# Cross-attention in a three-stage decoder block: scores issued in one stretch, maxima subtracted inside the second by-key block, projection behind the shift, gelus first

## The chip, the cores and the metric

One core of one Trainium2 chip. The metric is the device time of the whole program in microseconds (us); for the kernel before it is the median of three runs.

## The reference, cut to what matters

A decoder layer on `x` [64, 128, 128] with the context `ctx` [64, 77, 128], all in float32: self-attention, cross-attention, and an expert feed-forward network, each behind a layernorm and added to `x`. The change is in the cross-attention alone:

```python
def xattn(query, key, value, ...):            # query: layernorm(x), key = value: ctx
    Q, K, V = linear(query, Wq, bq), linear(key, Wk, bk), linear(value, Wv, bv)   # 16 heads of 8
    qk = einsum('bhqd,bhkd->bhqk', Q, K)
    scores = qk / sqrt(dk)
    mean_sim = scores.mean(axis=(-2, -1))
    max_sim = scores.max(axis=-1).mean(axis=-1)
    probs = softmax(scores, axis=-1)
    entropy_proxy = var(probs, axis=-1, ddof=1).mean(axis=-1)
    feats = stack([mean_sim, max_sim, entropy_proxy], axis=-1)
    hidden = gelu(linear(feats, w1, b1)); hidden = gelu(linear(hidden, w2, b2))
    t = exp(clip(linear(hidden, w3, b3), LOG_T_MIN, LOG_T_MAX))[..., None]
    attn = softmax(qk / (2.0 * t), axis=-1)
    return linear(einsum('bhqk,bhkd->bhqd', attn, V), Wo, bo)
```

So every head of every batch needs its scores twice: once for three features, from which a small MLP makes a temperature, and once with that temperature for the attention proper.

## The kernel before, in words

The three stages run one after the other. In the cross-attention one batch (128 queries by 77 keys, 16 heads) is a work item, and a software pipeline runs over the steps `n` of `STEPS`. In step `n` the engines work on these batches, with `LAG` = 7:

- batch `n + 2`: transposes of the normalised `x` and of the context (`xc_transpose`), the products Q, K and V (`qkv`), and their copies on ACT (`qkv_copy`) and casts on DVE (`cast`) and POOL (`low`, `key_masks`);
- batch `n`: first scores, queries on partitions, in the PSUM tile `SQ` of three banks (`scores_outer`, `scores_inner`), row maxima on DVE (`row_max`), their transpose (`max_transpose`), negated on ACT (`mT_copy`), subtracted in PSUM by three matmuls (`subtract_max`), exponentials on ACT (`exp_e`), sums on DVE;
- batch `n - 7`: second scores, keys on partitions, in `SK` of two banks, eight heads at a time (`by_key(b, 0)` and `by_key(b, 1)`): two matmuls put in the shift (`pick`, `shift`), six add the products; then the exponential on ACT (`exps(b, h)`, into `P`) and the product with V (`pv(b, h)`);
- batch `n - 8`: `o_copy`, `o_transpose`, `norm`, `on_transpose`, `onT_copy`;
- batch `n - 9`: `project` (bias matmul and output matrix) and `residual`.

`SK` exists once. So `by_key(b, 1)` waits for `exps(b, 0)`, and `by_key(b + 1, 0)` for `exps(b, 1)`: `need(pe, p_ready, 2 * b + h)`, L1273. `SQ` exists once as well; `scores_outer` waits for the exponentials of the batch before (`e1_ready`).

Once in four steps (`mlp_round(n)`, n = 5, 9, ..., 65) the MLP of four batches runs: `mlp1`, `gelu1`, `mlp2`, `gelu2`, `mlp3`, `bound`, `inverse_t`, `factors`. Exponential and gelu need different tables in ACT, so that such a step has two table loads.

Every product in float32 is made of three parts (high by high, high by low, low by high). The scores' matmuls use 32 of the 128 rows: group `g` of four heads lies on rows `32g` to `32g + 31` of the keys and queries (masked per head). The 16 heads stand in `SQ` six, six and four to a bank, so that heads 4 to 7 are cut into two pieces, and the outer groups write heads 0 to 3, 8 to 11 and 12 to 15. The inner ones may start only behind them (`outer_ps`), since the first matmul into a bank clears its flags.

The order of the work on each engine is written out by hand in the loop over `STEPS` at the end of each engine's block; PE takes its instructions from one queue, and each function's waits stand at its head. While the pipeline fills (n from 2 to 6) and at its end (n from 64), `filler` puts matmuls without a use on PE.

## Time and profile before

| | us |
|---|---|
| median of three runs | 1720.15 (1714.52 to 1722.27) |
| the profiled execution | 1719.28 |
| its span | 1717.5 |
| cross-attention, by the first transposes on PE and the last projection | from 484.5 to 1159.9 |

| engine | busy us | share of the span |
|---|---|---|
| PE (matmul) | 1642.8 | 96% |
| DVE | 1235.7 | 72% |
| ACT | 926.2 | 54% |
| POOL | 880.2 | 51% |

A share is an average over three stages. To read the change, one looks at the cross-attention alone, at one step and at one round of four steps, and at which wait ends last there. PE's ends are modelled, so a busy PE may still hold gaps; the starts of its rows tell more than its busy time. The granted clock of TensorE is 1.0 at full speed (2.4 GHz) and 0.5 at half (1.2 GHz).

### The profile page before, as it was taken

The page shows a single profiled execution, that of the slowest core. Times are in us where ns is not written, and L with a number is a line of the kernel's source. Part 1 is how long each engine was busy: PE and PEld are TensorE (multiplying, and loading weights), DVE is VectorE, ACT ScalarE, POOL GpSimd, SP SyncE. Part 2 cuts the span into 40 slices and gives each one's busy share as a digit, 9 for nine tenths or more (in the row PEclk, how much of TensorE's full clock was granted, in tenths as well). Part 3 has the DMA queues.
Part 4 walks back from the last instruction along what each step waited for, and adds up shares of the span by engine and source line. Part 5 has one row for each costly group of instructions (what it writes and reads, how often), then busy time and mean ns, then how long its engine had stood idle before and what let it go on. Part 6 is the DMA issues. An engine that isn't in the chain of part 4 may idle for free. (4 is left out here: it accounts for less than half of the span.)

```text
span 1717.5 us, 42620 instructions
## 1 busy us (share of the span) xinstructions
PE 1642.8 (96%) x14336; PEld 1223.2 (71%) x14336; DVE 1235.7 (72%) x2888; ACT 926.2 (54%) x2189; POOL 880.2 (51%) x1006
## 2 busy tenths in 40 slices
PE   6999999999978999999999999897999999999998
PEld 2555555555546666666666666557999999999998
DVE  5887777777646767766677776436878878787886
ACT  3555545555433666666566666545454545545452
POOL 3444455544446767776677777412433434343342
PEclk9999999999958999998999999788999999999999
DMA  4000000000000000000000000100000000000000
GB/s 123 13 3 2 1 1 1 1 1 1 6 5 4 7 7 7 6 7 6 6 7 7 7 7 5 43 2 1 11 6 9 6 9 6 9 9 6 9 6 13
DMA packets 27869, 16.62 MB, mean 10 GB/s; under 512 B 6193, under 2 KB 25586, under 8 KB 27762
## 3 DMA queue, kind: packets, MB, share of 16 engines
q1 hardware_dynamic: 27762, 15.23, 3.2%
q8 instruction: 63, 1.03, 0.3%
q14 instruction: 44, 0.36, 0.1%
HBM read 9.97 MB, written 4.19 MB: 8 GB/s over the span
## 5 line engine op out<-in xcount | busy, mean ns | idle before, releaser
L1555 POOL TENSOR_TENSOR ff_zz<-ff_zt 128x256 f32<-128x256 f32 x32 | 37.5, 1173 | 318.2 <-DVE ff_zt L1759 318.2
L278 POOL TENSOR_TENSOR sa_KM<-sa_HQK,sc_headmask 128x512 fp32r<-128x512 f32 x64 | 66.7, 1042 | 235.6 <-ACT sa_HQK L318 235.6
L964 ACT ACTIVATE xa_P<-xa_SK 77x1024 f32<-77x1024 f32 x128 | 130.2, 1017 | 98.1 <-PE xa_SK L1287 97.9
L1623 ACT ACTIVATE ff_SG<-bank 128x512 f32<-128x512 f32 x128 | 76.6, 599 | 189.3 <-PE bank L1836 189.3
L1749 DVE TENSOR_TENSOR ff_GL<-ff_GU,ff_GH 128x512 fp32r<-128x512 f32 x128 | 148.6, 1180 | 27.2 <-ACT ff_GH L1628 27.2
L323 ACT ACTIVATE sa_P<-sa_SK 128x1024 f32<-128x1024 f32 x128 | 131.5, 1028 | 59.1 <-PE sa_SK L515 59.1
L409 DVE TENSOR_REDUCE sa_mx<-sa_SQ 128x8 f32<-128x1024 f32 x128 | 156.7, 1224 | 7.6 <-PE sa_SQ L515 5.3
L890 POOL TENSOR_TENSOR xa_QMH<-xa_QBH,xc_headmask 128x512 fp32r<-128x512 f32 x64 | 72.6, 1135 | 151.2 <-ACT xa_QBH L954 151.2
L1901 PE MATMUL bank<-fh_r,ff_GH 128*128 128x256 f32 x512 | 149.2, 292 | 0.0
L1834 PE MATMUL bank<-ff_ZH,fh_b 128*128 128x256 f32 x512 | 146.2, 286 | 0.0
L1903 PE MATMUL bank<-fh_r,ff_GL 128*128 128x256 f32 x512 | 144.5, 282 | 0.0
L1902 PE MATMUL bank<-fl_r,ff_GH 128*128 128x256 f32 x512 | 144.4, 282 | 0.0
L1836 PE MATMUL bank<-ff_ZH,fl_b 128*128 128x256 f32 x512 | 143.8, 281 | 0.0
L1835 PE MATMUL bank<-ff_ZL,fh_b 128*128 128x256 f32 x512 | 143.2, 280 | 0.0
L849 POOL TENSOR_TENSOR xa_E<-xa_E 128x1232 f32<-128x1232 f32 x64 | 143.2, 2238 | 0.0
L1744 DVE TENSOR_TENSOR ff_GU<-ff_SG,bank 128x512 f32<-128x512 f32 x128 | 88.1, 688 | 64.4 <-ACT ff_SG L1623 58.7
L1628 ACT CAST ff_GH<-ff_GU 128x512 fp32r<-128x512 f32 x128 | 79.0, 623 | 56.3 <-DVE ff_GU L1744 33.1
L1080 DVE TENSOR_REDUCE xa_FEAT<-xa_SQ 128x12 f32<-128x924 f32 x64 | 71.7, 1120 | 42.0 <-PE xa_SQ L1236 41.7
L1563 POOL TENSOR_TENSOR ff_ZH<-ff_AH,ff_M 128x512 fp32r<-128x512 f32 x64 | 83.4, 1303 | 34.3 <-ACT ff_M L1601 34.3
L534 PE MATMUL sa_SK<-sa_shift,sa_pick_row 128*128 128x512 f32 x256 | 99.9, 471 | 0.7 <-ACT sa_P L323 0.6
L1902 PEld LDWEIGHTS bank<-fl_r,ff_GH 128*128 128x128 f32 x512 | 97.4, 190 | 0.0
L1901 PEld LDWEIGHTS bank<-fh_r,ff_GH 128*128 128x128 f32 x512 | 97.2, 190 | 0.0
(259 smaller groups left out, 5398.3 us busy)
## 6 DMA issues: line engine op xcount, KB each, us to landing
xa_shift<-xa_row SPq DMA_DIRECT2D x256, 2.0 KB
out<-X SPq DMA_DIRECT2D x64, 64.0 KB, 1.5
cx<-ctx SPq DMA_DIRECT2D x64, 38.5 KB
sa_shift<-sa_mT SPq DMA_DIRECT2D x64, 8.0 KB, 1.8
X<-x SPq DMA_DIRECT2D x1, 768.0 KB, 6.7
xa_E<-L_ffn_B SPq DMA_DIRECT2D x2, 256.0 KB, 3.7
xa_E<-down_a SPq DMA_DIRECT2D x1, 512.0 KB, 4.4
X<-x SPq DMA_DIRECT2D x1, 256.0 KB, 2.9
```

What stands on the lines that cost most here:

```text
L323: nc.scalar.activation(P[:, 2 * (k % 2) + h, :], SK[:], ACT.Exp).then_inc(p_ready, 1)
L409: nc.vector.tensor_reduce(mx[:, p, 2 * JH * h:2 * JH * h + 2 * JH], SQ[:].rearrange("q (j k) -> q j k", k=T), AX.X, ALU.max).then_inc(max_ ...
L534: mm(bank(SK, a), pick_row[:], shift[:, k % 2, JH * g:JH * g + JH, :].rearrange("c j t -> c (j t)"), start=True, stop=False)
L849: nc.gpsimd.tensor_tensor(E2[:], E1[:, b % 2], E1[:, b % 2], ALU.mult).then_inc(e2_ready, 1)
L964: nc.scalar.activation(P[0:TC, (2 * b + h) % 4, :], SK[0:TC, :], ACT.Exp).then_inc(p_ready, 1)
L1749: nc.vector.tensor_tensor(GG[1][:, k % 4, :], GU[:, k % 2, :], GG[0][:, k % 4, :].bitcast(F32), ALU.subtract).then_inc(gl_done, 1)
L1834: mm(out, w[0], x[0], start=start, stop=False, **kw)
L1835: mm(out, w[0], x[1], start=False, stop=False, **kw)
L1836: return mm(out, w[1], x[0], start=False, stop=stop, **kw)
L1901: mm(out, h, RD[0][:, f, :], start=(s == 0 and f == 0), stop=False, skip_group_check=True)
L1902: mm(out, h, RD[1][:, f, :], start=False, stop=False, skip_group_check=True)
L1903: last = mm(out, l, RD[0][:, f, :], start=False, stop=(s == 1 and f == 3), skip_group_check=True)
```

## The change

- The constant `CROSS_ORDER` = (2, 1, 3, 0) gives the group of heads that stands at each place of `SQ`. Groups 2 and 3 are now the first and third place, group 1 is the one cut in two, and group 0 has the last bank. `headsel` and the four rows of the shift that SP copies are put in the same order; the number of DMAs stays at four.
- PE: the first scores are one stretch. `scores_outer` holds places 0 and 2 (six matmuls), `scores_inner` begins with the first matmul of place 3, waits for `outer_ps`, and holds the other eight. It moves ahead of the transposes of batch `n + 2`.
- PE: `pv(n - 8, 1)` moves from behind the outer scores to behind those transposes; `project` from the head of the step into `by_key(n - 7, 0)`, behind its shift matmuls; `max_transpose` out of `by_key(n - 7, 1)` to ahead of it; `subtract_max` into it, behind its shift matmuls.
- PE: `mlp1`, `mlp2` and `mlp3` stand behind the scores, behind the transposes and behind `pv(n - 8, 1)`.
- ACT: in a step with MLP both gelus stand ahead of `exps(n - 7, 0)`; in every step `scaled` is first, and `exp_e` and `onT_copy` stand ahead of `exps(n - 7, 1)`.
- DVE: `residual` behind `sum_e`, `bound` ahead of `stats`, `layernorm` ahead of `cast`, `factors` ahead of `sum_e2`, `norm` at one place in all steps.
- The fillers of a step while the pipeline fills: four, three and two where it had four and six.

```diff
+CROSS_ORDER = (2, 1, 3, 0)
...
-                for g in range(QUADS):
+                for place, g in enumerate(ORDER):
                     sp.dma_start(shift[32 * g:32 * g + 1, b % 2].bitcast(F32),
-                                 row[JH * g:JH * g + JH].bitcast(F32)).then_inc(m_row[b % 2], 16)
+                                 row[JH * place:JH * place + JH].bitcast(F32)).then_inc(m_row[b % 2], 16)
...
                 r = mlp_round(n)
-                if real(n - LAG):
-                    exps(n - LAG, 0)
                 if real(n - LAG + 1):
                     scaled(n - LAG + 1)
+                if r is not None:
+                    gelu1(r)
+                if real(n - LAG) and r is None:
+                    exps(n - LAG, 0)
                 if real(n + 2):
                     xcT_copy(n + 2)
                 if r is not None:
-                    gelu1(r)
+                    gelu2(r)
                 if real(n - LAG - 1):
                     o_copy(n - LAG - 1)
-                if r is not None:
-                    gelu2(r)
+                if real(n - LAG) and r is not None:
+                    exps(n - LAG, 0)
                 if real(n):
                     mT_copy(n)
                 if real(n + 2):
                     qkv_copy(n + 2)
+                if r is not None:
+                    inverse_t(r)
+                if real(n):
+                    exp_e(n)
+                if real(n - LAG - 1):
+                    onT_copy(n - LAG - 1)
                 if real(n - LAG):
                     exps(n - LAG, 1)
-                if r is not None:
-                    inverse_t(r)
-                if real(n - LAG - 1):
-                    onT_copy(n - LAG - 1)
-                if real(n):
-                    exp_e(n)
...
                 for part in range(3):
-                    scores(b, 0, 4, part, part == 0, part == 2)
-                    scores(b, 8, 12, part, part == 0, part == 2)
-                    last = scores(b, 12, 16, part, part == 0, part == 2)
+                    scores(b, 0, 4, part)
+                    last = scores(b, 8, 12, part)
                 last.then_inc(outer_ps, 1)
 
             def scores_inner(b):
+                scores(b, 12, 16, 0)
                 pe.wait_ge(outer_ps, b + 1)
                 for part in range(3):
-                    scores(b, 4, 6, part, False, part == 2)
-                    last = scores(b, 6, 8, part, False, part == 2)
+                    if part > 0:
+                        scores(b, 12, 16, part)
+                    scores(b, 4, 6, part)
+                    last = scores(b, 6, 8, part)
                 last.then_inc(sq_ps, 1)
...
                 for a, _, r in quads:
                     mm(bank(SK, a), pick[:, r // 32], shift[:, b % 2].rearrange("c j t -> c (j t)"),
                        start=True, stop=False)
+                between()
                 for part, (keys, queries) in enumerate(((HK, QMH), (HK, QML), (LK, QMH))):
...
-                if real(n - LAG - 2):
-                    project(n - LAG - 2)
...
                 if real(n - LAG):
-                    by_key(n - LAG, 0)
+                    by_key(n - LAG, 0, project_last)
+                else:
+                    project_last()
                 if real(n):
                     scores_outer(n)
-                if real(n - LAG - 1):
-                    pv(n - LAG - 1, 1)
+                    scores_inner(n)
                 if r is not None:
                     mlp1(r, n)
                 if real(n + 2):
                     xc_transpose(n + 2)
-                if real(n):
-                    scores_inner(n)
+                if r is not None:
+                    mlp2(r)
+                if real(n - LAG - 1):
+                    pv(n - LAG - 1, 1)
+                elif 2 <= n < LAG:
+                    filler(SK[:, 512:1024], 3)
+                if r is not None:
+                    mlp3(r)
                 if real(n + 2):
                     qkv(n + 2)
...
+                if real(n):
+                    max_transpose(n)
                 if real(n - LAG):
-                    by_key(n - LAG, 1, maxima)
+                    by_key(n - LAG, 1, subtract)
```

Where the instructions stand now, first on PE, in a step without MLP of the steady part: around the second by-key block (into `xa_SK`). Before, from the transposes of o (`o_transpose`, into `xa_R`) to the projection:

```order
L1321 MATMUL xa_R<-fc_ident,xa_o 128x128 x2
L1283 MATMUL xa_SK<-xa_shift,xa_pick 128x512 x2
L1287 MATMUL xa_SK<-xa_QMH,xa_HK 128x512 x2
L1261 MATMUL xa_O<-fc_ident,xa_FEAT 16x128
L1287 MATMUL xa_SK<-xa_QML,xa_HK 128x512 x2
L1287 MATMUL xa_SK<-xa_QMH,xa_LK 128x512 x2
L1268 MATMUL xa_SQ<-xa_heads,xa_mT 128x462 x2
L1268 MATMUL xa_SQ<-xa_heads,xa_mT 128x308
L1326 MATMUL xa_R<-fc_ident,xa_on 128x128
L1305 MATMUL xa_O<-xa_P,xa_VA 32x128 x8
L1333 MATMUL xa_M<-xa_bias,xa_minus_ones 128x128
L1334 MATMUL xa_M<-xc_wo,xa_onT 128x128
```

With the change, from behind those transposes to the projection inside the next step's block:

```order
L1267 MATMUL xa_O<-fc_ident,xa_FEAT 16x128
L1289 MATMUL xa_SK<-xa_shift,xa_pick 128x512 x2
L1274 MATMUL xa_SQ<-xa_heads,xa_mT 128x462 x2
L1274 MATMUL xa_SQ<-xa_heads,xa_mT 128x308
L1294 MATMUL xa_SK<-xa_QMH,xa_HK 128x512 x2
L1294 MATMUL xa_SK<-xa_QML,xa_HK 128x512 x2
L1294 MATMUL xa_SK<-xa_QMH,xa_LK 128x512 x2
L1331 MATMUL xa_R<-fc_ident,xa_on 128x128
L1310 MATMUL xa_O<-xa_P,xa_VA 32x128 x8
L1289 MATMUL xa_SK<-xa_shift,xa_pick 128x512 x2
L1338 MATMUL xa_M<-xa_bias,xa_minus_ones 128x128
L1339 MATMUL xa_M<-xc_wo,xa_onT 128x128
```

The transpose of the maxima (into `xa_O`) left the block and stands ahead of it, the three subtracting matmuls (into `xa_SQ`) moved in behind the shift, and the projection (into `xa_M`) moved from between `pv` and the next block to behind that block's shift.

Then the first scores (into `xa_SQ`) of the same kind of step on PE, from the last row of `by_key(n - 7, 0)`. Before:

```order
L1287 MATMUL xa_SK<-xa_QMH,xa_LK 128x512 x2
L1236 MATMUL xa_SQ<-xa_KMH,xa_HQ 128x308 x3
L1236 MATMUL xa_SQ<-xa_KML,xa_HQ 128x308 x3
L1236 MATMUL xa_SQ<-xa_KMH,xa_LQ 128x308 x3
L1305 MATMUL xa_O<-xa_P,xa_VA 32x128 x8
L1217 MATMUL xa_M<-fc_ident,xa_xn 128x128
L1218 MATMUL xa_M<-fc_ident,cx 128x77
L1236 MATMUL xa_SQ<-xa_KMH,xa_HQ 128x154 x2
L1236 MATMUL xa_SQ<-xa_KML,xa_HQ 128x154 x2
L1236 MATMUL xa_SQ<-xa_KMH,xa_LQ 128x154 x2
```

With the change:

```order
L1294 MATMUL xa_SK<-xa_QMH,xa_LK 128x512 x2
L1240 MATMUL xa_SQ<-xa_KMH,xa_HQ 128x308 x2
L1240 MATMUL xa_SQ<-xa_KML,xa_HQ 128x308 x2
L1240 MATMUL xa_SQ<-xa_KMH,xa_LQ 128x308 x2
L1240 MATMUL xa_SQ<-xa_KMH,xa_HQ 128x308
L1240 MATMUL xa_SQ<-xa_KMH,xa_HQ 128x154 x2
L1240 MATMUL xa_SQ<-xa_KML,xa_HQ 128x308
L1240 MATMUL xa_SQ<-xa_KML,xa_HQ 128x154 x2
L1240 MATMUL xa_SQ<-xa_KMH,xa_LQ 128x308
L1240 MATMUL xa_SQ<-xa_KMH,xa_LQ 128x154 x2
L1221 MATMUL xa_M<-fc_ident,xa_xn 128x128
L1222 MATMUL xa_M<-fc_ident,cx 128x77
```

The 15 matmuls stand together, with those of group 0 (the last place, 308 columns) between those of group 1 (154 columns each); `pv` and the transposes follow them.

And ACT in a step with MLP, from its first instruction on. Before:

```order
L964 ACTIVATE xa_P<-xa_SK 77x1024
L954 ACTIVATE xa_QBH<-xa_QK,xa_cfc 128x128
L957 ACTIVATE xa_row<-xa_mT,xa_cfh 16x128
L915 COPY xa_xcT<-xa_M 128x205
L978 ACT_TABLE_LOAD
L978 ACTIVATE xa_h<-xa_R,xa_b1s 64x64
L969 COPY xa_o<-xa_O 128x256
L982 ACTIVATE xa_h<-xa_R,xc_b 64x64
L937 ACTIVATE xa_mT<-xa_O 16x128
L922 ACTIVATE xa_QK,xa_qsum<-xa_M,xc_bq 128x128
L924 ACTIVATE xa_QK,xa_ksum<-xa_M,xc_bk 128x77
L931 COPY xa_VA<-xa_M 77x2x8x8
```

With the change:

```order
L958 ACTIVATE xa_QBH<-xa_QK,xa_cfc 128x128
L961 ACTIVATE xa_row<-xa_mT,xa_cfh 16x128
L982 ACT_TABLE_LOAD
L982 ACTIVATE xa_h<-xa_R,xa_b1s 64x64
L919 COPY xa_xcT<-xa_M 128x205
L986 ACTIVATE xa_h<-xa_R,xc_b 64x64
L973 COPY xa_o<-xa_O 128x256
L968 ACT_TABLE_LOAD
L968 ACTIVATE xa_P<-xa_SK 77x1024
L941 ACTIVATE xa_mT<-xa_O 16x128
L926 ACTIVATE xa_QK,xa_qsum<-xa_M,xc_bq 128x128
L928 ACTIVATE xa_QK,xa_ksum<-xa_M,xc_bk 128x77
```

Both gelus (`xa_h`) stand ahead of the first exponential of `SK` (`xa_P`), and the second one is behind the exponentials of `SQ` (`xa_E`) and the copy `xa_onT`, of which the rows above show all but the end.

## Rows read from the trace of the kernel before

**Rows 1.** One round: length, busy us of PE, PEld, DVE, ACT, POOL; granted clock.

```profile
852.29:889.53 37.24, 35.61 (x335) 23.91 (x335) 26.85 (x57) 24.91 (x66) 27.09 (x34) 1.00 0.03 7
```

**Rows 2.** PE in order of time, three places: start us, us, engine, line, operation.

```profile
584.15 0.32 PE L1333 MATMUL xa_M<-xa_bias,xa_minus_ones 2*128 2x128 f32 x1 [0.77 <-ACT xa_onT L974]
...
695.18 1.38 PE L1268 MATMUL xa_SQ<-xa_heads,xa_mT 128*128 128x462 f32 x3
...
1076.58 0.47 PE L1333 MATMUL xa_M<-xa_bias,xa_minus_ones 2*128 2x128 f32 x1
```

**Rows 3.** PE in order of time, one step without MLP (899.24 to 906.69).

```profile
899.24 0.50 PE L1287 MATMUL xa_SK<-xa_QMH,xa_HK 32*128 32x512 f32 x2
899.35 0.41 PE L1236 MATMUL xa_SQ<-xa_KMH,xa_HQ 32*128 32x308 f32 x2
899.58 0.40 PE L1287 MATMUL xa_SK<-xa_QML,xa_HK 32*128 32x512 f32 x2
...
899.83 0.39 PE L1236 MATMUL xa_SQ<-xa_KMH,xa_LQ 32*128 32x308 f32 x2
...
900.55 0.64 PE L1305 MATMUL xa_O<-xa_P,xa_VA 128*32 128x128 f32 x16
...
901.45 0.45 PE L1236 MATMUL xa_SQ<-xa_KMH,xa_HQ 32*128 32x154 f32 x2
...
902.27 0.49 PE L1222 MATMUL xa_M<-xa_xcT,xc_wq 128*128 128x128 f32 x2
...
903.14 0.70 PE L1283 MATMUL xa_SK<-xa_shift,xa_pick 128*128 128x512 f32 x2
...
904.20 0.28 PE L1261 MATMUL xa_O<-fc_ident,xa_FEAT 128*16 128x128 f32 x1
904.41 0.50 PE L1287 MATMUL xa_SK<-xa_QML,xa_HK 32*128 32x512 f32 x2
...
905.07 0.83 PE L1268 MATMUL xa_SQ<-xa_heads,xa_mT 128*128 128x462 f32 x3
905.74 0.27 PE L1326 MATMUL xa_R<-fc_ident,xa_on 128*128 128x128 f32 x1
...
906.69 0.32 PE L1333 MATMUL xa_M<-xa_bias,xa_minus_ones 2*128 2x128 f32 x1
```

**Rows 4.** ACT in order of time, the end of the same step.

```profile
906.40 0.24 ACT L974 COPY xa_onT<-xa_R 128x128 f32<-128x128 f32 x1
...
907.38 0.40 ACT L946 ACTIVATE xa_E<-xa_SQ 128x308 f32<-128x308 f32 x1
```

**Rows 5.** PE in order of time, a by-key block alone, behind the last scores.

```profile
1138.31 0.70 PE L1283 MATMUL xa_SK<-xa_shift,xa_pick 128*128 128x512 f32 x2
...
1139.83 0.33 PE L1326 MATMUL xa_R<-fc_ident,xa_on 128*128 128x128 f32 x1
```

**Rows 6.** PE and ACT in order of time, the step with MLP at 881.

```profile
881.08 0.56 PE L1344 MATMUL xa_R<-xa_FEAT,xa_w1s 128*64 128x64 f32 x6
...
882.36 1.28 ACT L978 ACT_TABLE_LOAD   x1
...
883.65 0.31 ACT L978 ACTIVATE xa_h<-xa_R,xa_b1s 64x64 f32<-64x64 f32 x1
...
883.86 0.35 ACT L969 COPY xa_o<-xa_O 128x256 f32<-128x256 f32 x1
...
884.01 0.43 PE L1349 MATMUL xa_R<-xa_h,xa_w2p 64*128 64x64 f32 x2 [0.40 <-ACT xa_h L978]
...
889.53 0.32 PE L1333 MATMUL xa_M<-xa_bias,xa_minus_ones 2*128 2x128 f32 x1 [0.81 <-ACT xa_onT L974]
```

**Rows 7.** ACT in order of time, the last step with MLP, where ACT waits.

```profile
1110.61 1.28 ACT L964 ACT_TABLE_LOAD   x1
1113.05 1.02 ACT L964 ACTIVATE xa_P<-xa_SK 77x1024 f32<-77x1024 f32 x1 [1.16 <-PE xa_SK L1287]
```

**Rows 8.** PE in order of time, the first step with MLP, while the pipeline fills.

```profile
539.31 0.90 PE L1344 MATMUL xa_R<-xa_FEAT,xa_w1s 128*64 128x64 f32 x6 [2.51 <-POOL xa_FEAT L869]
```

65 lines of the change are left out of this document (29 added, 36 removed).

## The prediction

> **What bounds the kernel now.** The page of the profile says PE 96% busy over the span. The stretches by stage are read next. In one undisturbed round of four steps PE is busy 35.61 of 37.24 us, the next engine, POOL, 27.09 [rows 1]; DVE and ACT lie near it. So PE's one queue sets the pace, and the others count only where PE waits for them. Then PE in order of time: a step without MLP takes 8.58 (889.53 to 906.69 are two) [rows 3, 6], and it has almost no gap. The round leaves 37.24 - 3 x 8.58 = 11.50 for the step with MLP, whose gaps the list of waits names: 0.40 for the first gelu and 0.81 for the copy `onT` [rows 6]. So the change is read on PE's queue: which instructions get closer together, and which of PE's new places is reached before the result it needs.
>
> The sum is made against the profiled execution, 1719.28 (span 1717.5), 0.9 under the median 1720.15. I reckon one step, from the end of one by-key block to the end of the next, and multiply: steps 7 to 63 are full, 14 of them with MLP and 43 without.
>
> **a. Scores in one stretch.** Before, from the first product of `by_key(b, 0)` to `pv` 1.31 (899.24 to 900.55), and the inner scores 0.82 (901.45 to 902.27): 2.13 [rows 3]. The first is that long because group 0 of the scores shares its rows with the by-key block and comes last. Now groups 2 and 3 run beside the block: such a pair starts at 899.35, 0.11 behind the block's first, the last pair at 899.83 with 0.39 to its end, 900.22 [rows 3]. The inner scores must wait for that end; before, `pv` and the transposes covered it. With 0.05 for the semaphore (a gelu ends at 883.96, its matmul starts at 884.01 [rows 6]) they start at 900.27 and take 0.82; group 0's matmuls run on other rows beside group 1's. So 899.24 to 901.09, 1.85: **-0.28**. Bounds: nothing gained, 2.13 (0); or no wait and a tighter pace, 1.65 (-0.48: start at 900.05, half the gaps of group 1 filled, 0.84). I take 1.85, since its two parts are rows.
>
> The trace shows scores starting (899.35) ahead of the second by-key product (899.58), which stands before them in the program [rows 3]. The Trainium skill, TensorE: Matmul & The Clock Gate, section "Part 3: Packing small matmuls", says that matmuls start and end strictly in program order, whatever their row groups. By that the pairs would queue up behind the block and the stretch would give nothing; the trace disagrees, and the measurement decides.
>
> **b. Maxima out of the second block.** Before, from its shift to the subtraction 1.93 (903.14 to 905.07), with the transpose of the maxima inside, which waits for both row groups to run empty [rows 3]. A block alone takes 1.52 (1138.31 to 1139.83) [rows 5]. The transpose itself still costs 0.21 (904.20 to 904.41) [rows 3]. 1.52 + 0.21 - 1.93 = **-0.20**. The subtraction only changes its place. Is the transpose reached too early? From the inner scores to it were 2.75 us (901.45 to 904.20) [rows 3]; now transposes 0.33, `pv` 0.57, `qkv` with `o_transpose` 0.87 and the 0.82 themselves give 2.59. A wait of up to 0.16 is possible; the 2.75 were partly the drain, so I book none.
>
> **c. Projection behind the shift.** The same instructions in another order, one change to 32 rows either way: 0. Its wait for `onT` goes.
>
> **d. What is late next.** The shift of `by_key(b + 1, 0)` overwrites `SK` and needs `exps(b, 1)`. Before, ACT did that exponential at once behind the block, and subtraction, `on_transpose`, `pv` and projection covered it. Now ACT has `exp_e` and `onT_copy` ahead of it, and PE has only `on_transpose` and one `pv` to do. The chain from the start of `on_transpose`: 0.27 [rows 3], 0.05, the copy 0.24 [rows 4], the exponential 1.02 [rows 7] less 0.10 of overlap (a copy starts at 883.86, 0.10 ahead of the end of the gelu [rows 6]), 0.05: 1.53. Before, from `on_transpose` to the next instruction 0.95 (905.74 to 906.69) [rows 3]. **+0.58** a step; PE stands still for some 0.75 of it. `exp_e` itself fits between: copy and both its parts take 1.38 (906.40 to 907.78) [rows 4], so 1.24 from the end of the subtraction, while the products of the block take 0.89 and `on_transpose` 0.3. ACT's order here undoes what a and b save.
>
> Step without MLP: -0.28 - 0.20 + 0.58 = +0.10, so 8.68; 43 x 0.10 = **+4.3**.
>
> **e. Step with MLP.** Add to 8.68: `mlp1` 0.56; the first gelu, 0.05 + 0.31 + 0.05 behind it, of which the transposes cover 0.33: 0.08; `mlp2` 0.43 [rows 6], `mlp3` as much. The gelu's table load of 1.28 [rows 6] is now hidden: a load does not wait for its instruction's semaphore (at 1110.61 it ran at once, its exponential waited for PE until 1113.05 [rows 7]), and ACT is idle there until the MLP starts. The other load moves ahead of `exps(b, 0)`, and the second block's shift waits for that: from the end of `pv`, ACT needs 0.05 + 0.35 (copy of o) + 1.28 + 1.02 + 0.05 = 2.75, PE has `mlp3` 0.43, 0.87 and 0.21 to do; a stall of 1.24. Together 8.68 + 1.50 + 1.24 = 11.42 against 11.50; 14 x -0.08 = **-1.1**. One stall has taken the place of the two.
>
> **f. Filling and emptying.** Seven steps without by-key: the scores' saving holds, 7 x -0.28 = -2. In step 5 PE stood 2.51 before `mlp1` [rows 8], and the inner scores behind it; now they are ahead: -2.5. The ten steps behind the last scores hold the same chain d: +1. The fillers are 5 instead of 6 in the middle of a step and cost nothing, since PE waits there. DVE's new order: it has 26.85 of 37.24 us to do [rows 1]; SP's DMAs keep number and place: 0. **-3.5**.
>
> **g. Clock.** The 13 rounds from 584.15 to 1076.58 take 492.4 [rows 2], 13 x 37.24 are 484.1: 8.3 more than the undisturbed round gives. In such rounds rows stand at half speed at the end of the step with MLP: the subtraction at 695.18 shows 1.38 where 905.07 has 0.83 [rows 2, 3]. PE had waited before it, and matmuls of 64 columns ran. With the MLP in one run and its weak stretch broken up by `pv`, I estimate that half of it goes: **-4**, with -8 and the rival below as its bounds.
>
> The Trainium skill, same page, section "Part 1: The HAM clock gate", puts the half rate down to a stretch in which the engine was idle. By that the kernel before would lose nothing, for no gap in a round exceeds 0.81 [rows 6], and g would be 0. The rows disagree.
>
> Sum: 4.3 - 1.1 - 3.5 - 4 = -4.3, so 1719.3 - 4.3 = **1715**.
>
> **The rivals.**
> - **The scores pack tighter (faster).** If the stretch takes 1.65 instead of 1.85, 57 x -0.20 = -11.4: **1704**. For it: pairs of different groups start 0.11 apart, and group 1 alone leaves gaps. Against it: the wait for `outer_ps` is now in the open.
> - **Half clock on the path (slower).** PE's standstill of 1.24 is followed by subtraction, block and `on_transpose`, which all lie on chain d. At half speed the subtraction takes 0.55 more [rows 2, 3] and the rest about as much again by its 0.89: 1.2 a round, where before the wait for `onT` hid most of it. 15 rounds give 18, and the 4 of g are lost as well: **1737**. It decides where most rounds have it. For it: the step holds one gap longer than any before, and each step a second one of 0.75. Against it: `pv`, with full rows, stands right before the gap.
> - **No overlap in the stretch (slower).** Groups 0 and 1 take turns or the wait is long: 2.13, so +0.28 x 57 = 16: **1731**. By the page's rule of program order it would be this one; the pairs at 899.35 speak against it.
>
> **How the numbers follow.** Forecast 0.46, first rival 0.29, second 0.17, third 0.08. A measurement tells about 0.5% from no change, 8.6 us: faster is under 1711.5, slower over 1728.7. The forecast's own spread (0.16 of a wait in b, 0.05 here or there in d, a few us of clock) is 1709 to 1723; a little of it is faster, and the first rival nearly all: 0.32. The second and third give slower, less some that stop short: 0.22. Same: 0.46. The range reaches from below the first rival, with the clock's gain on top, to just short of the second: 1700 to 1735; some 2 in 10, mostly half clock, lie outside.
>
> **What the profile after would show.** Steps without MLP of 8.68; PE's shift at the head of a step waiting some 0.75 for `xa_P` (`exps(b, 1)`); in the step with MLP one wait of 1.2 for `xa_P` at the second block, and no wait above 0.2 for a gelu; from the first by-key product to the transposes of `x` 1.85. A step of 8.5 or less with 1.65 there is the first rival, 8.9 with 2.1 the third; subtractions of 1.38 in most rounds the second. If PE shows no wait for `xa_P` at the head of a step, d is wrong, and with it the forecast: it would then be some 30 us too high.

## The result and the profile after

| | before | after |
|---|---|---|
| median | 1720.15 (beside the changed kernel 1720.8) | 1777.01 |
| runs | 1714.52 to 1722.27 | 1776.23, 1755.99, 1802.93, 1777.79 |
| profiled execution | 1719.28, span 1717.5 | 1776.23, span 1774.4 |

The ratio of after to before is 1.0293, with a 95% interval of 1.02 to 1.0387: slower, by something between 2 and 4%. The forecast was 1715, its range 1700 to 1735; the time lies 42 above the range. A run over 1.5% above the fastest of its kernel, like that of 1802.93, is not part of a ratio, here and below.

The page of the profile of the changed kernel: span, busy times, and the granted clock in 40 slices of the span (tenths).

```profile
span 1774.4 us, 42623 instructions
...
PE 1664.5 (94%) x14337; PEld 1239.6 (70%) x14337; DVE 1231.9 (69%) x2888; ACT 941.9 (53%) x2189; POOL 872.8 (49%) x1006
...
PEclk9999999999968799999798888897999999999999
```

PE has 94% instead of 96%, and the clock row holds 6, 7 and 8 in ten slices between the 12th and the 28th, where the cross-attention runs. Two causes are possible, then: the order and the clock. The stretches tell them apart. First one undisturbed round of the changed kernel (the answer to [rows 1]), then a stretch of 560 us in the middle of the cross-attention, then a piece of it; the columns are those of [rows 1], with the granted clock after the engines:

```profile
896.75:935.47 38.72, 34.54 (x335) 23.19 (x335) 26.19 (x56) 25.98 (x65) 26.58 (x35) 1.00 0.03 7
...
560.00:1120.00 560.00, 514.02 (x4432) 346.65 (x4432) 349.29 (x743) 346.66 (x867) 355.25 (x455) 0.88 0.02 6
...
994.00:1011.10 17.10, 16.39 (x91) 11.35 (x91) 7.75 (x20) 8.04 (x18) 6.29 (x7) 0.50 0.01 3
```

The same 560 us of the kernel before:

```profile
560.00:1120.00 560.00, 542.69 (x4843) 362.40 (x4842) 383.08 (x803) 360.41 (x925) 388.16 (x484) 0.94 0.03 9
```

The round takes 38.72 instead of 37.24 us at full clock, with 34.54 instead of 35.61 of PE busy. And the mean clock is 0.88 against 0.94: half-speed time is twice the missing part, (1 - 0.88) x 2 x 560 = 134 us against 67. The trace's own record of the clock gives 133 and 70 for the same 560 us, and where half-speed time is given from here on, it is from that record and for these 560 us of the profiled execution. It comes in whole spells, as from 994.0 to 1011.1, where the clock is 0.50 throughout.

PE in order of time at either end of 13 rounds, as in [rows 2]:

```profile
587.32 0.47 PE L1338 MATMUL xa_M<-xa_bias,xa_minus_ones 2*128 2x128 f32 x1
...
1136.19 0.47 PE L1338 MATMUL xa_M<-xa_bias,xa_minus_ones 2*128 2x128 f32 x1
```

That is 548.9 us; before it was 492.4. An undisturbed round, one at full clock throughout, is 11.76 + 3 x 8.99 = 38.73 (the one above has 38.72). Of the +56.5, 13 x (38.73 - 37.24) = **+19.4 is the order**, and what is left, **+37.1, the clock**: 548.9 stands 45.4 above 13 undisturbed rounds, before it was 8.3. The spans differ by 56.9, so all that lies outside these 13 rounds changed by 0.4.

The size of the clock's part holds for the profiled execution alone. Its mean clock is 0.936 over the whole span; the run of 1755.99 had 0.955, close to the 0.957 of the profiled execution before, and still took 37 us longer than that one. Half-speed time is also dearer in this kernel: within the 13 rounds 132 us of it cost 45.4, before 51 us cost 8.3.

**Where the spells begin.** `mlp1` starts at 991.49 in the round of the spell above, and the clock falls 2.4 us later. PE behind the fall, at the second by-key block:

```profile
996.27 1.22 PE L1289 MATMUL xa_SK<-xa_shift,xa_pick 128*128 128x512 f32 x2 [0.46 <-ACT xa_P L968]
```

So in this round the wait for `exps(b, 0)` comes 2 us behind the fall and can't have brought it. Six of the eleven spells that begin in the 560 us (92 of the 133 us) start in this way, 1.4 to 2.5 us behind the start of `mlp1`; the other five start at other places.

**A step without MLP**, PE in order of time (it answers to [rows 3]):

```profile
926.49 0.32 PE L1338 MATMUL xa_M<-xa_bias,xa_minus_ones 2*128 2x128 f32 x1
...
927.16 0.50 PE L1294 MATMUL xa_SK<-xa_QMH,xa_HK 32*128 32x512 f32 x2
927.18 0.41 PE L1240 MATMUL xa_SQ<-xa_KMH,xa_HQ 32*128 32x308 f32 x2
...
927.50 0.39 PE L1294 MATMUL xa_SK<-xa_QML,xa_HK 32*128 32x512 f32 x2
927.57 0.30 PE L1240 MATMUL xa_SQ<-xa_KMH,xa_LQ 32*128 32x308 f32 x2
...
928.27 0.40 PE L1240 MATMUL xa_SQ<-xa_KML,xa_HQ 32*128 32x308 f32 x1
...
929.09 0.33 PE L1221 MATMUL xa_M<-fc_ident,xa_xn 128*128 128x128 f32 x1
...
930.71 0.38 PE L1326 MATMUL xa_R<-fc_ident,xa_o 128*128 128x128 f32 x2
...
930.96 0.71 PE L1289 MATMUL xa_SK<-xa_shift,xa_pick 128*128 128x512 f32 x2
931.56 0.82 PE L1274 MATMUL xa_SQ<-xa_heads,xa_mT 128*128 128x462 f32 x3
...
933.20 0.33 PE L1331 MATMUL xa_R<-fc_ident,xa_on 128*128 128x128 f32 x1
...
934.80 0.74 PE L1289 MATMUL xa_SK<-xa_shift,xa_pick 128*128 128x512 f32 x2 [0.70 <-ACT xa_P L968]
935.47 0.32 PE L1338 MATMUL xa_M<-xa_bias,xa_minus_ones 2*128 2x128 f32 x1
```

935.47 - 926.49 = 8.98 (8.97 to 9.00 in the undisturbed steps without MLP) where the forecast was 8.68 and before 8.58. In pieces, before against after:

| piece | before | after | change | forecast |
|---|---|---|---|---|
| by-key and all scores | 1.31 + 0.82 | 1.93 (927.16 to 929.09) | -0.20 | -0.28 |
| `o_transpose` to `on_transpose`: maxima, second block, subtraction | 2.74 | 2.49 (930.71 to 933.20) | -0.25 | -0.20 |
| `project` and the first shift | 1.12 | 0.66 + 0.67 | +0.21 | 0 |
| `on_transpose` to the next head | 0.95 | 1.60 (933.20 to 934.80) | +0.65 | +0.58 |

The row of the third piece in the kernel before, the shift and the first product behind `project` (906.69, [rows 3]):

```profile
907.18 0.70 PE L1283 MATMUL xa_SK<-xa_shift,xa_pick 128*128 128x512 f32 x2
907.81 0.50 PE L1287 MATMUL xa_SK<-xa_QMH,xa_HK 32*128 32x512 f32 x2
```

The wait at the head is in the list of waits (total us, times, longest; 700 to 1150 us), with the MLP steps' larger one in the same row:

```profile
PE xa_SK L1289 <- ACT xa_P L968: 34.7, 52, 1.3
```

Of the 52, 37 are of 0.70 and 4 of 1.31; the other 11, of 0.3 to 0.5, stand where PE runs at half speed and so comes later.

ACT in order of time at the end of that step shows the chain behind it: the two parts of `exp_e` (the first is shown), the copy `onT`, `exps(b, 1)`.

```profile
932.42 0.94 ACT L949 ACTIVATE xa_E<-xa_SQ 128x924 f32<-128x924 f32 x1
...
933.57 0.27 ACT L978 COPY xa_onT<-xa_R 128x128 f32<-128x128 f32 x1
933.73 1.02 ACT L968 ACTIVATE xa_P<-xa_SK 77x1024 f32<-77x1024 f32 x1
```

**The step with MLP** at 905.74 takes 11.76 (before 11.50). ACT, in order of time (it answers to [rows 6]); then PE at the second by-key block:

```profile
905.61 1.28 ACT L982 ACT_TABLE_LOAD   x1
908.93 0.31 ACT L982 ACTIVATE xa_h<-xa_R,xa_b1s 64x64 f32<-64x64 f32 x1 [2.03 <-PE xa_R L1349]
...
910.75 1.28 ACT L968 ACT_TABLE_LOAD   x1
912.04 1.02 ACT L968 ACTIVATE xa_P<-xa_SK 77x1024 f32<-77x1024 f32 x1
```

```profile
911.53 0.27 PE L1267 MATMUL xa_O<-fc_ident,xa_FEAT 128*16 128x128 f32 x1
913.12 0.73 PE L1289 MATMUL xa_SK<-xa_shift,xa_pick 128*128 128x512 f32 x2 [1.31 <-ACT xa_P L968]
```

The gelu's table load runs at 905.61, while ACT waits for `mlp1` anyway, and the list of PE's waits has none for a gelu any more. The second load stands ahead of `exps(b, 0)`, and PE waits 1.31 for that exponential.

### The profile page after: what moved, and what is told of

The parts are those of the page before. It is cut to its first block and busy times, and to the rows that moved or that the text cites. A ratio compares the mean times of both kernels' runs of the same rounds, so it can differ in the third digit from the quotient of the medians.

```text
span 1774.4 us, 42623 instructions
## 1 busy us (share of the span) xinstructions
PE 1664.5 (94%) x14337; PEld 1239.6 (70%) x14337; DVE 1231.9 (69%) x2888; ACT 941.9 (53%) x2189; POOL 872.8 (49%) x1006
## 5 line engine op out<-in xcount | busy, mean ns | idle before, releaser
L1289 PE MATMUL xa_SK<-xa_shift,xa_pick 128*128 128x512 f32 x256 | 103.1, 487 | 52.4 <-ACT xa_P L968 51.4
L878 POOL TENSOR_TENSOR xa_LK<-xa_QK,xa_HK 128x77 fp32r<-128x77 f32 x64 | 21.7, 340 | 164.3 <-DVE xa_HQ L1079 164.3
L1289 PEld LDWEIGHTS xa_SK<-xa_shift,xa_pick 128*128 128x128 f32 x256 | 43.3, 212 | 77.8 <-ACT xa_P L968 75.4
```

Source lines behind the costliest of these rows:

```text
L1289: mm(bank(SK, a), pick[:, r // 32], shift[:, b % 2].rearrange("c j t -> c (j t)"), start=True, stop=False)
```

## The experiments

Fifteen kernels ran, in four lots, each beside the kernel before (whose medians in these were 1716.8, 1714.6, 1721.6 and 1720.0). Times are medians, with the ratio to before. First those that undo one part, on the changed kernel.

**e1: projection back at the head of its step.**

```diff
+                project_last()
...
                 if real(n - LAG):
-                    by_key(n - LAG, 0, project_last)
-                else:
-                    project_last()
+                    by_key(n - LAG, 0, lambda: None)
```

> The changed kernel with one thing undone: the projection stands again at the head of the step, ahead of the first by-key block, not behind its shift. Theory A (the order costs 0.4 a step because the exponential exps(b, 1) comes late, PE has nothing to do meanwhile, and the projection inside the block costs 0.49 plus a drain of 0.18 on the path): the projection moves into the wait of 0.70, steps without MLP go from 8.98 to 8.31, a round from 38.7 to 36.1, so some 13 x 2.6 = 34 us less than the changed kernel, and 1705 to 1740 by what the clock does. Theory B (the clock alone is the loss): the steps at full clock matter little, the spells at half speed stay, about 1770. Rival C (the scores in one stretch are the loss): steps stay near 8.9.

Measured 1703.8, 0.995 (0.9896 to 1.0003). The step is 8.31 or 8.32, as worked out, the MLP step 11.10. PE in order of time, from `on_transpose` over `project` and the shift to the first product:

```profile
932.15 0.33 PE L1331 MATMUL xa_R<-fc_ident,xa_on 128*128 128x128 f32 x1
...
932.99 0.32 PE L1338 MATMUL xa_M<-xa_bias,xa_minus_ones 2*128 2x128 f32 x1
...
933.76 0.74 PE L1289 MATMUL xa_SK<-xa_shift,xa_pick 128*128 128x512 f32 x2
934.42 0.49 PE L1294 MATMUL xa_SK<-xa_QMH,xa_HK 32*128 32x512 f32 x2
```

That is 2.27, against 2.93 in the changed kernel (933.20 to 936.14) and 2.07 before: the matmuls of `project` now stand where PE waited for `exps(b, 1)`, and nothing stands between shift and products. So `project` in this place costs 0.66 a step. Part c, booked at nothing, is 0.21 of it; the other 0.45 is wait that `project` no longer covers, and that was in the price of d. Half-speed time is 58 us. The list of waits:

```profile
PE xa_SK L1289 <- ACT xa_P L968: 15.1, 12, 1.3
```

Eleven of the twelve waits left are the MLP steps' stall (1.31). It is as long as in the changed kernel, and yet the record of the clock has five spells instead of eleven. Against the kernel before, e1 is not clear of noise: its interval reaches 1.

**e2: ACT does `exps(b, 1)` first, then `onT`, then `exp_e`** (the order before). **e3: both edits.**

```diff
+                if real(n - LAG):
+                    exps(n - LAG, 1)
+                if real(n - LAG - 1):
+                    onT_copy(n - LAG - 1)
                 if real(n):
                     exp_e(n)
-                if real(n - LAG - 1):
-                    onT_copy(n - LAG - 1)
-                if real(n - LAG):
-                    exps(n - LAG, 1)
```

> The changed kernel with another thing undone: on ACT exps(n - 7, 1), onT_copy, exp_e in the order of the kernel before. Theory A: from the start of on_transpose to the next shift 1.19 (0.12 + 1.02 + 0.05) where it is 1.60, so 0.41 less a step, 8.57, and 20 to 25 us less than the changed kernel at equal clock. Theory B: no change beyond the clock's scatter, about 1770. If exp_e comes too late for the next scores, part of the 0.41 comes back as a wait of the scores.

> Both undone at once: projection at the head of the step and ACT's old order. Theory A: the projection now waits for onT_copy, which stands behind the exponential, from the start of on_transpose 1.04 + 0.24 + 0.05 = 1.33, then 0.66 of projection: 1.99 to the shift, where the first of the two alone has 1.60; steps of 8.7, so slower than the projection alone by 0.4 a step, near the kernel before, 1720 to 1730. If two parts of a loss simply added, it would be the fastest of the three.

e2: 1736.8, 1.0139 (1.0077 to 1.02), step 8.57, half-speed time 81 us. The head's wait falls from 0.70 to 0.28. e3: 1718.6, 1.0003 (0.9985 to 1.002), step 8.52. There PE waits for the other copy, at `project`:

```profile
933.65 0.32 PE L1338 MATMUL xa_M<-xa_bias,xa_minus_ones 2*128 2x128 f32 x1 [0.43 <-ACT xa_onT L978]
```

So d is real, but ACT's old order helps only where the projection stands inside the block. With the projection in front the changed kernel's ACT order is the better one by 0.21 a step.

**e4: twelve narrow matmuls (128 columns) in the MLP step's stall.**

```diff
-                    mm(where, pick[:, 0], heads[:, 0:512], start=True, stop=True)
+                    mm(where, pick[:, 0], heads[:, 0:where.shape[-1]], start=True, stop=True)
...
                     o_transpose(n - LAG - 1, r)
+                    if r is not None and n < B:
+                        filler(O[:, 3 * T:4 * T], 12)
```

> The changed kernel with 12 matmuls of 128 columns without a use on PE, in the steps with MLP only, between the transposes of o and that of the maxima, where PE then waits 1.3 for exps(b, 0). They fill a wait and add no more than 0.3 of path to a step. Theory D (the spells at half clock, 37 of the 57 us, come from that wait in the MLP step): the spells become few, rounds of 38.7 throughout, about 1740. Rival E (they come from the 0.70 of wait in every step, or from the sparse matmuls of the MLP ahead of the wait): the spells stay, 1765 to 1780.

1763.3, 1.0259 (1.0219 to 1.0298); clock 0.90 over the 560 us. The spells are others (two of over 20 us, one of 14, eight of 7), 112 us in all. The stall is not the cause by itself, which agrees with the spells of the changed kernel that begin ahead of it.

**e5: three full-width matmuls (512 columns) in the wait at the head of every step.**

```diff
+                if LAG < n < B:
+                    pe.wait_ge(v_sb, n + 2 if n + 2 < B else B)
+                    filler(M[:, 0:512], 3)
                 if real(n - LAG):
```

> The changed kernel, with three full-width idle products of 512 columns (into M, free there) at the head of each step, in the 0.70 us in which PE waits for exps(b, 1). They take 3 x 0.21 at full clock and fit into the wait, so at full clock the step stays 8.99 and the MLP step 11.76. Theory A (the half clock comes from the waits of every step, which make PE's work thin over the whole round): half-speed time falls from 133 us to 60 or less, about 1740. Theory B (it comes from the stretch of the MLP step alone, its stall of 1.3 and the narrow matmuls about it): no change in the spells, 17 us in each round or every other, 1765 to 1778. Were the fillers on the path after all (shift delayed by 0.1 to 0.2 a step), steps of 9.1 to 9.2 would show it.

1736.6 (all four runs within 1736.4 to 1738.9), 1.013 (1.0106 to 1.0153). PE in order of time at a head:

```profile
929.56 0.96 PE L1318 MATMUL xa_M<-xa_heads,xa_pick 128*128 128x512 f32 x3
930.36 0.71 PE L1289 MATMUL xa_SK<-xa_shift,xa_pick 128*128 128x512 f32 x2
```

The fillers start at 929.56, the shift at 930.36 without a wait, and step (8.99) and MLP step (11.77) are what they were. The clock over 560 us:

```profile
560.00:1120.00 560.00, 537.51 (x4858) 359.08 (x4857) 369.74 (x782) 365.96 (x909) 374.41 (x477) 0.97 0.02 6
```

31 us at half speed instead of 133, and 40 us less in the median (28 by the ratios to the kernel before, 1.0293 and 1.013). This is the clock's part of the change, taken away without touching the order: what stays, 1736.6 against 1714.6, is 22 us, where the order gives 43 x 0.40 + 14 x 0.27 = 21 over all full steps. As e5 has less half-speed time than the kernel before, too (31 against 70), the order may be worth a few us more than that.

**e6 and e7: `exps(b, 0)` ahead of the gelus in MLP steps too**, e6 on the changed kernel, e7 on e1.

```diff
+                if real(n - LAG):
+                    exps(n - LAG, 0)
                 if r is not None:
                     gelu1(r)
-                if real(n - LAG) and r is None:
-                    exps(n - LAG, 0)
...
-                if real(n - LAG) and r is not None:
-                    exps(n - LAG, 0)
```

> The changed kernel, with exps(b, 0) ahead of the first gelu on ACT in MLP steps too, as before: the stall of 1.3 us at the second by-key block goes, and the gelu's table load of 1.28 comes back behind exps, so that mlp2 waits. Worked out: exps ends 1.07 behind its block, load to 2.35, while mlp1 ends at about 1.7: mlp2 late by 0.65 to 0.7 instead of the 1.3. MLP step 11.76 - 0.6 = 11.15, 14 x -0.6 = -9. Theory B (the one long stall brings the half clock): spells nearly gone, 1776 - 9 - 37 = 1730. Theory A (each step's 0.70 brings it, thinning the whole round): spells stay, some 100 us or more of half speed, 1765.

> e1 (the changed kernel with the projection back at the head of its step, 1703.8) with the edit of e6 besides. Steps without MLP stay at 8.31; the MLP step loses its stall of 1.3 and gets a wait of 0.7 for the first gelu: 11.10 - 0.6 = 10.5, 14 x -0.6 = -8: 1695, and up to 10 less if the rest of the half-speed time (58 us in e1) goes with the stall. If the inverse_t exponential or xcT_copy comes too late instead, the MLP step stays at 11.1 and the time at 1704.

Both missed: e6 1820.5, 1.0602 (1.0568 to 1.0636), e7 1738.1, 1.0155 (1.0116 to 1.0194). The wait for the gelu is 0.89 where I reckoned 0.7, and a second one came that I had left out. PE in e6, in order of time:

```profile
803.47 0.43 PE L1352 MATMUL xa_R<-xa_h,xa_w2p 64*128 64x64 f32 x2 [0.89 <-ACT xa_h L982]
...
811.90 1.22 PE L1287 MATMUL xa_SK<-xa_shift,xa_pick 128*128 128x512 f32 x2 [1.59 <-ACT xa_P L968]
```

ACT in between:

```profile
808.09 1.28 ACT L991 ACT_TABLE_LOAD   x1
```

The load back to the exponential's table now stands behind the copies of Q, K and V, right in the chain of `exp_e`, `onT` and `exps(b, 1)`, so the next head waits 1.59 instead of 0.70 (1.3 to 2.0 in the other rounds). Taking `exps` ahead didn't remove the load, it moved it to a worse place. The MLP step is 12.48 where 11.15 was worked out and 11.76 stood, which makes 14 x 0.72 = 10 us; the clock fell to 0.82 over the 560 us (197 us at half speed). So with ACT's half of "gelus first" taken back the changed kernel loses another 43 us, some 30 of it clock. In e7 the steps without MLP stay at 8.32, but the MLP step is 11.67 (10.5 worked out, 11.10 in e1) and half-speed time 118 us. Given PE's new order, the gelus have to be first on ACT; what they bring against the kernel before, forecast as 1.1, these two runs don't tell.

Now the parts by themselves, on the kernel before.

**b1: all scores in one stretch. b3: the same, with `pv(b, 1)` behind the transposes of x.** Both have the order of the head groups, of `scores` and of the constants from the change.

```diff
                     scores_outer(n)
+                    scores_inner(n)
-                if real(n - LAG - 1):
-                    pv(n - LAG - 1, 1)
                 if r is not None:
                     mlp1(r, n)
                 if real(n + 2):
                     xc_transpose(n + 2)
-                if real(n):
-                    scores_inner(n)
+                if real(n - LAG - 1):
+                    pv(n - LAG - 1, 1)
```

(b1 leaves `pv` where it was.)

> The kernel before with only part a: all score matmuls in one stretch, the rest of every engine's order as it was. The changed kernel's trace showed 1.93 from the first by-key product to the transposes of x (forecast 1.85), so the price of a alone should be 1.93 - 2.13 = -0.20, if what surrounds it does not matter: steps without MLP of 8.38 (before 8.58), MLP step 11.3, and 57 x -0.20 = -11: 1706. If it pays only together with the other parts (the pv that stood between the two halves now stands behind them, and the transposes of x still follow): steps of 8.5 to 8.58, 1713 to 1717. Half-speed time as before, 75 us or less between 560 and 1120.

> The kernel before with part a and pv(b, 1) moved behind the transposes of x, so that the copy xcT is covered again (b1 had left it open: a wait of 0.42 a step). Steps without MLP of 8.58 - 0.20 = 8.38; MLP step 11.3 to 11.9 (the gelu's table load is reached 0.8 earlier than before, so its wait grows from 0.4 to about 0.7, as b1 showed). At full clock 43 x -0.20 + 14 x 0 = -9: 1707. Theory A (waits in the plain steps bring the half clock; here there are none): half-speed time 75 us or less, 1700 to 1710. Theory C (it is the MLP step's waits for gelus, which b1, e6 and e7 share, all of them with exps(b, 0) ahead of the gelu): half-speed time over 120 us, 1740 or more.

b1: 1799.1, 1.0507 (1.0443 to 1.0572), the worst but one of all. Its step is 8.86, since the inner scores had covered ACT's copy `xcT`:

```profile
929.90 0.49 PE L1222 MATMUL xa_M<-xa_xcT,xc_wq 128*128 128x128 f32 x2 [0.42 <-ACT xa_xcT L915]
```

The stretch itself takes 1.93 there as well. The longer step makes 43 x 0.28 = 12 us. Most of the 84 us is clock (the 560 us again, 192 of them at half speed, 92 in one spell):

```profile
560.00:1120.00 560.00, 525.99 (x4283) 341.68 (x4283) 333.95 (x718) 329.20 (x839) 347.44 (x440) 0.83 0.02 6
```

b3: 1734.1, 1.0085 (1.0054 to 1.0117). Steps of 8.41 agree with a's -0.20 (8.38 worked out), but the gain does not arrive: the 1707 is missed by 27 us. The profiled execution is the fastest of the four, 1720.96 with 62 us at half speed and a mean clock of 0.959; the others took up to 1739.4 with 0.945 to 0.953. So b3 met neither of its two theories. MLP steps stay at 11.5, since they reach the gelu, and then `project`, sooner than ACT:

```profile
925.07 0.43 PE L1351 MATMUL xa_R<-xa_h,xa_w2p 64*128 64x64 f32 x2 [0.65 <-ACT xa_h L978]
...
930.58 0.32 PE L1335 MATMUL xa_M<-xa_bias,xa_minus_ones 2*128 2x128 f32 x1 [0.81 <-ACT xa_onT L974]
```

**b2: maxima and subtraction as in the change** (and `mlp3`, which goes with the subtraction), nothing else. The cut leaves out that `by_key(b, 1)` now calls `subtract` behind its shift matmuls.

```diff
+                if real(n):
+                    max_transpose(n)
                 if real(n - LAG):
-                    by_key(n - LAG, 1, maxima)
+                    by_key(n - LAG, 1, subtract)
```

> The kernel before with part b alone: transpose of the maxima ahead of the second by-key block, subtraction (and mlp3) behind its shift. Forecast -0.20 a step; the changed kernel's trace shows 2.49 from o_transpose to on_transpose against 2.74 before, so -0.25: steps of 8.33, 57 x -0.25 = -14: 1702. Rival: before, the 2.75 us between the inner scores and the transpose of the maxima covered DVE's row maxima; now they are 2.3, and PE waits for max_ready: the gain goes, steps of 8.6, 1717. A second one: on_transpose comes right behind the block and waits for norm as in the changed kernel it did not: steps of 8.4 with a wait for xa_on.

1783.5, 1.0343 (1.0289 to 1.0397). The first rival held in its cause, the wait for the row maxima, not in its size: the step is 9.46, not 8.6. PE in order of time, at the transpose of the maxima and at the next `project`:

```profile
945.07 0.28 PE L1261 MATMUL xa_O<-fc_ident,xa_FEAT 128*16 128x128 f32 x1 [0.56 <-DVE xa_FEAT L1082]
...
948.70 0.32 PE L1333 MATMUL xa_M<-xa_bias,xa_minus_ones 2*128 2x128 f32 x1 [0.43 <-ACT xa_onT L974]
```

DVE's row maxima are not ready, and ACT's copy `onT` comes late behind them. MLP steps are shorter, 10.92 against 11.46 to 11.48 before; 43 x 0.88 - 14 x 0.55 leaves 30 of the 62 us for the order, so that the rest is clock again. Its half-speed time is 78 us in the 560, but 138 from 560 us to the end of the cross-attention (75 before, 154 with the change), which in the slower kernels lies well behind 1120. The -0.25 of b, then, needs something that stands beside it in the change; the scores in one stretch and DVE's new order are the candidates, and no run took them apart.

Then the clock, with e1 as the base.

**e8: e1 with five full-width matmuls in the MLP step's stall.**

```diff
                     o_transpose(n - LAG - 1, r)
+                    if r is not None and n < B:
+                        filler(O[:, 0:512], 5)
```

> e1 (projection back at the head of its step, 1703.8, 58 us at half speed between 560 and 1120) with five full-width idle products of 512 columns in the stall of 1.3 us of each MLP step (into bank O, ahead of the transpose of the maxima). 5 x 0.21 = 1.05 fits, so steps stay 8.31 and 11.10 at full clock. Theory A (half clock comes from PE's work being thin; full-width products in a wait cure it, as they did in e5): half-speed time under 30 us, 1692 to 1698. Theory B' (with the waits of the plain steps gone, what is left is noise of the chip that no filler changes): 1703 to 1705. If the fillers cost by the later transpose of the maxima (its copy, the subtraction), MLP steps of 11.4 and 1707 would show it.

**1691.6** (six runs, 1688.8 to 1700.2), 0.9839 (0.9814 to 0.9865): faster than both kernels, by medians 30 us faster than the one before and 85 than the changed one. It met its theory A (under 30 us at half speed: 24). Steps are 8.31, MLP steps 11.1, so the fillers (first row) cost nothing; the clock is 0.98 (second row, the 560 us):

```profile
908.91 1.39 PE L1318 MATMUL xa_O<-xa_heads,xa_pick 128*128 128x512 f32 x5
```

```profile
560.00:1120.00 560.00, 552.58 (x5109) 369.56 (x5109) 400.79 (x823) 387.89 (x949) 388.60 (x491) 0.98 0.03 9
```

**e9: e1 with the wait put in by itself**, by an ACT copy that nobody reads.

```diff
+                if real(n - LAG) and n < B:
+                    nc.scalar.activation(idle[:], heads[:, 0:400].bitcast(F32), ACT.Copy, scale=1.0)
                 if real(n - LAG):
                     exps(n - LAG, 1)
```

> e1 with the suspected wait put in by itself: an ACT copy of 128x400 (about 0.5 us, by the 0.42 of exp_e's 128x308) ahead of exps(b, 1), written to a tile nobody reads. PE's order is that of e1. The shift at the head of the step then waits some 0.5 longer: steps of 8.8, MLP steps of 11.1 to 11.6, at full clock 57 x 0.5 = +28: 1732. Theory A (a wait of this size in every step thins PE's work and brings the half clock): half-speed time rises from 58 us to over 100, and the time to 1750 to 1775. If the half clock hangs on where PE's instructions stand (projection inside the by-key block) and not on the wait: 58 us of half speed, 1732.

1736.0, 1.0086 (1.0063 to 1.0109). ACT in order of time, the added copy; PE's waits; the 560 us:

```profile
933.39 0.54 ACT L1030 ACTIVATE xa_idle<-xa_heads 128x400 f32<-128x400 f32 x1
```

```profile
PE xa_SK L1292 <- ACT xa_P L969: 30.4, 50, 1.3
```

```profile
560.00:1120.00 560.00, 514.75 (x4764) 344.71 (x4764) 384.77 (x791) 394.76 (x974) 383.77 (x483) 0.95 0.03 7
```

The step is 8.74 instead of 8.31, 57 x 0.43 = 25, and 1703.8 + 25 = 1728; the median is 8 above it, the profiled execution (1725.2) 3 below. By the ratios to the kernel before, which hold for each lot, e9 stands 1.4% or 23 us above e1, so that nothing is left for the clock. PE waits as often as in the changed kernel (50 times against 52, 30.4 us against 34.7), but half-speed time is 51 us, no more than in e1 (in the profiled execution, the fastest of the five, with a mean clock of 0.962; the other four have 0.951 to 0.955). The waits are not of the same size, though: 41 are of 0.5 (the changed kernel has 37 of 0.70) and 9 of 1.3. So a wait of 0.5 in every step does not bring the half clock in this order; one of 0.70 was not tried in it.

**e10, e11, e12: e5's fillers at the heads of some steps alone**, on the changed kernel: at the MLP step's (e10), at that of the step behind it (e11), at the other two (e12).

```diff
+                if LAG < n < B and r is not None:                        # e10
+                if LAG < n < B and mlp_round(n - 1) is not None:         # e11
+                if LAG < n < B and r is None and mlp_round(n - 1) is None:   # e12
+                    pe.wait_ge(v_sb, n + 2 if n + 2 < B else B)
+                    filler(M[:, 0:512], 3)
```

> The changed kernel with e5's three full-width products only at the head of the MLP steps, some 6 us ahead of the stall at the second by-key block. Spells of half clock begin at that stall (949.6, 994.0, 1038.4, 1082.7). Theory N (near: the clock falls where the wait at the step's head and the stall come close together): half-speed time falls as in e5, to under 60 us, 1736 to 1748. Theory W (whole round: each step's wait counts alike): a quarter of e5's gain of 40, so 1765 to 1770. Theory P (what stands behind the stall decides): no change, 1777.

> The same products only at the head of the step behind an MLP step, some 5 us behind the stall. Theory N: no change in how often a spell begins (1765 to 1777), though it may end sooner. Theory W: a quarter of e5's gain, 1765 to 1770. Theory P: as e5, 1736 to 1748.

> The same products only at the heads of the other two steps of each round. Theory N and theory P: no change, 1770 to 1777, spells as in the changed kernel. Theory W: half of e5's gain, 1755 to 1760.

e10: 1774.1, 1.0299 (1.024 to 1.0358), 113 us at half speed: no gain. e11: 1753.2, 1.0204 (1.017 to 1.0237), all four runs within 1749.9 and 1754.4, 68 us. e12: median 1780.0 over four runs from 1748.1 to 1807.1; 1.0209 (1.0151 to 1.0268), taken from the two of 1748.1 and 1759.4 alone; 96 us. With the changed kernel at 1.0293 and e5 at 1.013, the ratios give 0 for e10, 0.9% each for e11 and e12, and 1.6% for e5.

One head of four, that right behind the MLP step, is thus worth about half of what e5 gains, where equal shares would give a quarter; the other two heads together have the same in the two runs of e12's ratio, while e11 has it in all four. The interval of the changed kernel (1.02 to 1.0387) takes in e11 and e12, so their gain over it is not clear of noise; that of e11 over e10 just is. None of the three theories was met: e10 rules out N and, with e11, that all heads count alike (W), and e11 stays short of P's 1736 to 1748. The spells also move. The expectation of e10 places their start at the stall (949.6, 994.0); by the rows of the changed kernel they begin there 2 us ahead of it. In e10 no spell begins between `mlp1` and the second block any more, but eleven begin elsewhere. So there is no one place whose filling cures it.

## Why the prediction was wrong, point by point

- **a, scores in one stretch**: mechanism right, size 0.08 off, 1.93 instead of 1.85. The last outer pair ends sooner than reckoned (927.57 + 0.30 is 0.71 behind the block's first product, not 0.98), but the scores behind `outer_ps` start 0.40 behind that end (928.27) and not 0.05. From there to the transposes it is 0.82, as reckoned. PE's weight loads show the wait 43 times:

```profile
PEld xa_SQ L1240 <- PE xa_SQ L1240: 15.3, 43, 0.4
```

 Group 0's first matmul, on the rows of the block, runs in that time (up to 928.27), so how much of the 0.40 is the semaphore stays open. A score starts at 927.18, ahead of the by-key products at 927.50 that stand before it in the program, as before. The page's rule of strict program order for matmuls (the Trainium skill, TensorE: Matmul & The Clock Gate, "Part 3: Packing small matmuls") fails here as it did in [rows 3], and the third rival with it.
- **b, maxima**: right, -0.25 for -0.20; no wait for the maxima. That it doesn't hold alone (b2: PE waits 0.56 for the maxima) I had half seen, when I compared 2.75 with 2.59.
- **c, projection behind the shift: the first step that failed.** I said "the same instructions in another order", "0". Before, `project` took 0.49 to the shift (906.69 to 907.18) and the shift 0.63 to the first product on 32 rows (907.81), 1.12 together. Now `project` starts 0.66 behind the shift, and the first product on 32 rows 0.67 behind `project`, 1.33 together. So the move costs +0.21 a step by itself, and 0.66 with the wait that `project` had covered (e1). The prediction counted one change to 32 rows either way; it left out that `project` takes 0.18 longer ahead of products on 32 rows than ahead of the shift.
- **d, `exps(b, 1)` late**: right, stall of 0.70 for some 0.75, +0.65 for +0.58.
- Together +0.40 a step for the +0.10 forecast: 43 x 0.30 = 13 of the miss. This was not one large error but a, c and d off by 0.08, 0.21 and 0.07 to the same side, less b.
- **e, step with MLP**: its own part right. 11.76 is 8.98 + 2.78, forecast 8.68 + 2.74; the load is hidden, the stall is 1.31 for 1.24. That makes 14 x 0.34 = 5 of the miss, all but half a microsecond of it the plain step's error carried on.
- **f, filling and emptying**: -3.5 forecast, +0.4 measured, with half-speed time in it on both sides; not taken further.
- **g, clock: the second and larger step that failed.** Forecast -4, measured +37.1. The second rival named the half clock, but as something that follows PE's standstill of 1.24, and priced only subtraction, block and `on_transpose` at half speed, 1.2 a round. In six of the eleven spells the clock falls ahead of that standstill, and a spell, once begun, covers the rest of the MLP step and most of the next: disturbed rounds have 14.03 and 12.4 for those two where 11.76 and 8.99 stood, 5.7 a round. At 18 + 4 = 22 I gave it 0.17; its price was too low, and its cause is right in part at most.

13 + 5 + 4 + 41 = 63, and 1777 - 1715 = 62. With the clock as forecast the kernel would have come out at 1715 + 13 + 5 + 4 = 1737, and e5 measures 1737: just above the range. The order alone takes the forecast to the edge of its range, the clock far beyond it.

The Trainium skill, same page, "A second HAM failure mode: psum-queue depth-cycling", tells of a kernel whose engine idles briefly between groups of matmuls, often enough for the clock to go back and forth. I had weighed only the rule on one idle stretch. By this one the change would have been the dangerous case, and the changed kernel, e5, e8 and e11 agree with it: half-speed time falls when short waits are filled (133 to 31 us, 58 to 24 and 133 to 68). e9 sets it a bound: 41 waits of 0.5 and 9 of 1.3, and 51 us.

**What stays open.** Why the clock falls where it does. The changed kernel and e9 differ in the size of the wait (0.70, 0.5), in what stands next to it (in e9 `project` in front of it, in the changed kernel between the shift and the 32-row products) and in step length (8.98, 8.74). Size alone does not order the kernels: b1, with 0.42 a step in front of `qkv` and up to 0.7 for the gelu, has 192 us of half speed and e3, with 0.43 in front of `project` and 1.31 in the MLP step, 61. No run took these apart.

## What to carry to other kernels

An order is priced by what each instruction covers, not by its own length: moving `project` from where PE waits to where it doesn't cost 0.66 us a step, of which 0.21 came from its new neighbours alone. Where waits have been squeezed into many short gaps, put useless full-width products in them before judging the order: if the time falls, it was the clock, and the filler may as well stay (e8, the fastest here). And a bundle's parts are not its price: a and b alone lose 84 and 62 us, 12 and some 30 of them by longer steps, the rest, as far as half-speed time tells, by the clock; a table load taken from one place turns up in another. Last, look at when the clock falls before naming the wait that brought it.

## What was not expected of the hardware

- Twelve matmuls of 128 columns in a wait of 1.3 us did little for the clock (1763); three of 512 columns in each wait of 0.7 (1737), and five of 512 in the wait of 1.3 (e1 to e8, 1704 to 1692) a good deal more. The three differ in place and in kernel as well, and no run filled one and the same wait with both widths, so that it is not shown that the width decides.
- The clock can cost a kernel more than the order: half-speed time between 560 and 1120 us ranged from 24 (e8) to 197 (e6) in kernels of the same useful work. b1 has 192 of it, and between 700 and 1150 us no wait of PE above 0.7.
- A table load of 1.28 us doesn't wait for what its activation waits for: at 905.61 it ran at once, its gelu waited until 908.93.
